# A mixture-of-experts layer on one core: the residual is loaded in the expert stage and biased by VectorE, every pair has its own buffer, and the stores go out on GpSimd's queue

## The reference

```python
def _L0_cond_ref(x, q_left, q_right, spectral_gate):   # a linear map on the channels of each token
    ...
def _L0_ffn_ref(x, W_in, b_in, W_gate, b_gate, W1, b1, W2, b2, W_out, b_out):
    h = x @ W_in + b_in
    t = h.reshape(B * S, -1)
    logits = t @ W_gate + b_gate
    probs = jax.nn.softmax(logits, axis=-1)
    topv, topi = jax.lax.top_k(probs, TOP_K)
    topv = topv / jnp.sum(topv, axis=-1, keepdims=True)
    route = jnp.zeros_like(probs).at[jnp.arange(t.shape[0])[:, None], topi].set(topv)
    mid = jax.nn.relu(jnp.einsum('nd,edh->neh', t, W1) + b1)
    eout = jnp.einsum('neh,ehd->ned', mid, W2) + b2
    moe_out = jnp.einsum('ne,ned->nd', route, eout)
    out = moe_out.reshape(B, S, -1) @ W_out + b_out
    return out
x = x + _L0_ffn_ref(_L0_cond_ref(x, ...), ...)
```

## Time and profile before

| what | value |
|---|---|
| time, median of 3 runs | 589.87 us (589.3 to 590.82) |
| the profiled execution | 589.61 us, of which the span from the first to the last instruction is 587.8 us |
| TensorE busy | 535.3 us (91%) |
| VectorE, ScalarE, GpSimd busy | 354.5, 300.9 and 240.7 us |
| bytes moved | 64.70 MB, mean 110 GB/s |

### The profile page before, as it was taken

How to read it: one execution, slowest core, us unless ns; L and a number is a source line. 1 busy time by engine, 2 the same in 40 slices (tenths; PEclk the granted TensorE clock), 3 DMA queues, 4 the chain that set the end, 5 groups by cost and what they waited for, 6 DMA issues and landing times.

```text
span 587.8 us, 14218 instructions
## 1 busy us (share of the span) xinstructions
PE 535.3 (91%) x4458; PEld 463.9 (79%) x4459; DVE 354.5 (60%) x696; ACT 300.9 (51%) x534; POOL 240.7 (41%) x291
## 2 busy tenths in 40 slices
PE   1999947899999999999999999999999999963887
PEld 1666826798998998898998998998899988852665
DVE  5359643675774774774784784774564554625754
ACT  1266554765565565565665665663543543503443
POOL 3012235073373472473482472472432433229400
PEclk9899986999999999999999999999999999995999
DMA  6506362051251251251251241111111121195695
GB/s 163 171 19 241 110 218 77 18 192 54 64 180 55 71 179 46 80 167 49 86 164 45 94 154 48 48 55 42 55 55 38 55 55 38 38 321 180 209 293 178
DMA packets 40359, 64.70 MB, mean 110 GB/s; under 512 B 5943, under 2 KB 28156, under 8 KB 40316
## 3 DMA queue, kind: packets, MB, share of 16 engines
q1 hardware_dynamic: 31548, 39.51, 20.9%
q0 software_dynamic: 8768, 24.65, 13.4%
HBM read 45.53 MB, written 18.61 MB: 109 GB/s over the span
## 4 chain that ended last, share of the span: by engine, by line
PE 81%; DMA 7%; DVE 3%; ACT 2%; issue 2%; SPq 2%; POOL 2%; POOLq 1%; DVEq 0%; ACTq 0%
PE bank L1027 33%; PE bank L1010 12%; PE bank L1012 12%; PE bank L1011 12%; PE bank L909 4%; DMA w1s<-in_x 3%; PE bank L991 3%; DMA w1s<-y_by_choice 2%; POOL w1s L451 2%; PE bank L1060 1%; PE bank L891 1%; DVE w1s L855 1%; PE bank L881 1%; DMA z_by_token<-w1s 1%; PE bank L918 1%
## 5 line engine op out<-in xcount | busy, mean ns | idle before, releaser
L545 ACT ACTIVATE region<-bank,b1p,cbits 128x256 f32<-128x256 f32 x312 | 158.8, 560 | 184.5 <-PE bank L1012 168.3
L1027 PE MATMUL bank<-w2s,region 128*128 x1872 | 210.6, 273 | 0.0
L1027 PEld LDWEIGHTS bank<-w2s,region 128*128 128x128 f16 x1872 | 183.2, 98 | 20.8
L1010 PE MATMUL bank<-region,w1s 128*128 128x256 f16 x624 | 171.1, 274 | 0.3 <-DVE region L799 0.3
L1011 PE MATMUL bank<-region,w1s 128*128 128x256 f16 x624 | 171.0, 274 | 0.0
L1012 PE MATMUL bank<-region,w1s 128*128 128x256 f16 x624 | 171.0, 274 | 0.0
L429 POOL DMA_INDIRECT y_by_choice<-region,dst x78 | 84.8, 1087 | 208.2 <-DVE region L810 192.4
L820 DVE CAST region<-region 128x512 f16<-128x512 f32 x156 | 66.7, 428 | 78.5 <-ACT region L545 74.3
L822 DVE TENSOR_TENSOR region<-region 128x512 f16<-128x512 f32 x156 | 108.0, 692 | 5.4
L422 POOL DMA_INDIRECT region<-z_by_token,src x78 | 77.6, 995 | 28.4 <-issue 23.6
L810 DVE SCALAR_TENSOR_TENSOR region<-bank,cbits,b2b 128x256 f32<-128x256 f32 x78 | 34.1, 479 | 76.0 <-PE bank L1027 76.0
(11 more groups left out here) (194 smaller groups left out, 434.2 us busy)
## 6 DMA issues: line engine op xcount, KB each, us to landing
region<-in_L_ffn_W SPq DMA_DIRECT2D x16, 1024.0 KB
w1s<-y_by_choice SPq DMA_DIRECT2D x16, 512.0 KB, 4.3
w1s<-in_x SPq DMA_DIRECT2D x8, 512.0 KB, 8.6
z_by_token<-w1s POOLq DMA_DIRECT2D x16, 256.0 KB, 2.9
w1s<-in_x SPq DMA_DIRECT2D x4, 1024.0 KB, 9.9
out<-w1s SPq DMA_DIRECT2D x16, 256.0 KB, 2.6
region<-z_by_token,src POOLq DMA_INDIRECT x78, 2.8
y_by_choice<-region,dst POOLq DMA_INDIRECT x78, 2.6
```

Source lines behind the costliest of these rows:

```text
L545: m = s.activation(midf[:, b, c * TS:(c + 1) * TS], FB[b][:, c * TS:(c + 1) * TS], ACT.Relu, bias=b1p[:, bass.ds(r, 1), f:f + 1].rearrange ...
L1010: mm(o, w, xs[:, par, 0, k, :], start=(k == 0), stop=False)
L1027: last = mm(YB[par][:, h * D:(h + 1) * D], mids[:, par, l, b, c * TS + h * P:c * TS + (h + 1) * P], w2_at(e, w, f), start=(f == 0 and l == ...
```

## The change

x is loaded by SyncE as soon as the last weights are converted and 17 tiles have passed the second layer (`load_residual`). The four MB go to space that is free by then: the two raw weight buffers, and the weights of the rank that was computed first, in `w1s` and `w2s`. VectorE adds b_out in place, two pairs behind each of the tiles 30 to 37 (`add_bias`). All 16 pairs have their own buffers in the rest of `w1s` and `w2s`, and SyncE issues all 16 loads one after the other when the rows are scattered. GpSimd issues the stores. The loops of the output stage are written out.

```diff
+        def pairs(i):
+            at = fin1[:, i * SF:(i + 1) * SF] if i < NF1 else fin2[:, (i - NF1) * SF:(i - NF1 + 1) * SF]
+            return at.rearrange("p (t k d) -> p t k d", t=CT, k=K)
...
+        XC = NT // 4
+        xres = [region[:, RR:RR + XC * D], region[:, RR + XC * D:RR + 2 * XC * D],
+                w1s[:, 0].bitcast(f32).rearrange("p l k f -> p (l k f)"),
+                w2s[:, 0].bitcast(f32).rearrange("p l k f -> p (l k f)")]
...
+        XB0 = 30
...
-            sp.wait_ge(s_mp, 4 * NTILE)
-            for c in range(4):
-                t = slice(c * NT // 4, (c + 1) * NT // 4)
-                sp.dma_start(xall[:, t], x_t[:, t, :]).then_inc(s_xf, 16)
+            def load_residual():
+                sp.wait_ge(s_wl, 4 * E)
+                sp.wait_ge(s_yp, N // TS + 1)
+                for c in range(4):
+                    sp.dma_start(xres[c].rearrange("p (t d) -> p t d", t=XC), x_t[:, c * XC:(c + 1) * XC, :]
+                                 ).then_inc(s_xf[c], 16)
+            load_residual()
             sp.wait_ge(s_sc[0], 16 * H * ((NTILE + 1) // 2))
             sp.wait_ge(s_sc[1], 16 * H * (NTILE // 2))
-            for i in range(SL):
-                sp.dma_start(yin[:, i], y_t[:, i * CT:(i + 1) * CT]).then_inc(s_yi[i], 16)
-            with sp.Fori(0, NS // SL - 1) as j:
-                for q in range(SL):
-                    load(j * SL + (q + SL), q)
-                    store(j * SL + q)
-            for i in range(NS - SL, NS):
-                store(i)
+            for i in range(NS):
+                sp.dma_start(pairs(i), y_t[:, i * CT:(i + 1) * CT]).then_inc(s_yi[i], 16)
             sp.wait_ge(s_st, 16 * NS)
...
-            pool.wait_ge(s_late, 16 * 2)
-            pool.wait_ge(s_xf, 16 * 4)
-            combine(pool, add_bias)
+            for i in range(NS):
+                pool.wait_ge(s_o, i + 1)
+                pool.dma_start(out_t[:, i * CT:(i + 1) * CT, :], residual(i)).then_inc(s_st, 16)
...
+            def add_bias(i):
+                c, q = divmod(i, NS // 4)
+                if q == 0:
+                    dve.wait_ge(s_xf[c], 16)
+                v.tensor_tensor(residual(i), residual(i), bc(boutb[:].unsqueeze(1), [P, CT, D]), ALU.add
+                                ).then_inc(s_xb, 1)
...
             for a in range(NTILE):
                 tile(a, a % 2, a // GT)
+                for i in range(2 * (a - XB0), 2 * (a - XB0) + 2):
+                    if 0 <= i < NS:
+                        add_bias(i)
```

More of the change, by code:

```diff
@@ L249, in moe_program @@
         s_sc = [sem(f"rows_scattered{i}") for i in range(2)]
-        s_yi = [sem(f"pairs_loaded{i}") for i in range(SL)]
+        s_yi = [sem(f"pairs_loaded{i}") for i in range(NS)]
         s_y1 = sem("first_choice_scaled")
@@ L258, in moe_program @@
         s_o = sem("out_ready")
-        s_xf = sem("residual_loaded")
+        s_xf = [sem(f"residual_loaded{i}") for i in range(4)]
         s_st = sem("out_stored")
@@ L291, in tiles, with combine @@
                 step(a, a % 2, a // GT, a % GT)
-        def combine(eng, step):
-            for i in range(SL):
-                step(i, i, 0)
-            with eng.Fori(1, NS // SL) as j:
-                for q in range(SL):
-                    step(j * SL + q, q, j)
+        def combine(step):
+            for i in range(NS):
+                step(i, i % 2)
+        XB0 = 30
         @block.sync
@@ L837, in _ @@
             dve.wait_ge(s_tab, 1)
+            dve.wait_ge(s_late, 16 * 2)
             for a in range(NTILE):
                 tile(a, a % 2, a // GT)
+                for i in range(2 * (a - XB0), 2 * (a - XB0) + 2):
+                    if 0 <= i < NS:
+                        add_bias(i)
             y_out(NTILE - 1, 0)
@@ L844, in finish, with mix @@
                 dve.wait_ge(s_xb, i + 1)
-                t = bass.ds(i * CT, CT)
-                v.tensor_tensor(xall[:, t], bank[2 + par][:].rearrange("p (t d) -> p t d", t=CT), xall[:, t],
+                v.tensor_tensor(residual(i), bank[2 + par][:].rearrange("p (t d) -> p t d", t=CT), residual(i),
                                 ALU.add).then_inc(s_o, 1)
-            def mix(i, slot, j):
-                dve.wait_ge(s_yi[slot], (j + 1) * 16)
+            def mix(i, par):
                 dve.wait_ge(s_y1, i + 1)
-                if later(i, 2):
+                if i >= 2:
                     dve.wait_ge(s_zp, i - 1)
                 for t in range(CT):
-                    last = v.scalar_tensor_tensor(ztok[:, slot % 2, t, :], yin[:, slot, t, 1, :],
-                                                  route[:, 1, bass.ds(i * CT + t, 1)], y1r[:, slot % 2, t, :],
+                    last = v.scalar_tensor_tensor(ztok[:, par, t, :], pairs(i)[:, t, 1, :],
+                                                  route[:, 1, i * CT + t:i * CT + t + 1], y1r[:, par, t, :],
                                                   ALU.mult, ALU.add)
                 last.then_inc(s_z, 1)
-                if later(i, 2):
-                    finish(i - 2, slot % 2)
-            combine(dve, mix)
+                if i >= 2:
+                    finish(i - 2, par)
+            combine(mix)
             finish(NS - 2, 0)
@@ L1062, in project, with mix_t @@
                 last.then_inc(s_op, 1)
-            def mix_t(i, slot, j):
+            def mix_t(i, par):
                 pe.wait_ge(s_z, i + 1)
-                if later(i, 2):
+                if i >= 2:
                     pe.wait_ge(s_zt, i - 1)
@@ L1069, in mix_t @@
                     for k in range(KD):
-                        last = tr(bank[slot % 2][:, (t * KD + k) * P:(t * KD + k + 1) * P],
-                                  ztok[:, slot % 2, t, k * P:(k + 1) * P], ident[:])
+                        last = tr(bank[par][:, (t * KD + k) * P:(t * KD + k + 1) * P],
+                                  ztok[:, par, t, k * P:(k + 1) * P], ident[:])
                 last.then_inc(s_zp, 1)
-                if later(i, 1):
-                    project(i - 1, (slot + 1) % 2)
-            combine(pe, mix_t)
+                if i >= 1:
+                    project(i - 1, 1 - par)
+            combine(mix_t)
             project(NS - 1, (NS - 1) % 2)
```

45 lines of the change are left out of this document (19 added, 26 removed).

## The result

The changed kernel takes 580.84 us, the median of 5 runs (577.28 to 581.17), against 589.87 for the kernel before (588.55 to 590.82). The ratio is 0.984, with a 95% interval of 0.981 to 0.988: 9.0 us less in medians. Some executions of a kernel are slower as a whole, and medians and ratios leave them out (six of 22 of the kernel before, beside the first four experiments). The profiled execution is the fastest of the five, at 577.28, with a span of 575.5.

The account below looks back on a forecast made before the run. TensorE, busy for 535.3 of 587.8 us, was taken as the bound. Start 3.95 and pace 6.27 us less, last store 0.3 more, gave a span of 577.9, as a median 580.0; predicted 579.8, range 577.0 to 584.0.

Parts of the forecast that it names:

- the start: Output stage: the first finish comes 3.95 us earlier, at 541.05 instead of 545.00.
- the pace: Output stage: TensorE paces finishes at 2.22 us instead of 2.64, so 15 steps take 33.3 us, 6.27 less.
- the end: From the last finish to the end of the span: 2.84 us instead of 2.54, 0.3 more.
- The x load costs nothing: Expert stage: the early x load beside gathers and scatters costs 0, with 3.4 us of cover for a slow gather.
- The additions cost nothing: Expert stage: two VectorE additions per tile, 0.69 us each, fit in 1.48 us of idle time; cost 0.
- The hole: TensorE's idle time before the output stage: first transposes start 2.4 us earlier, at 535.2, second ones 3.95 us earlier.
- The clock's rise: Output stage: TensorE's clock rises to full 4.4 us after the second transposes start, at 540.9.
- The DMA rival: Second half of the output stage: DMAs set the pace, giving 582.3 or 584.4 us; chance 0.19.
- The stores on GpSimd: Output stage: issues take 0.73 us and only the last store's time counts, 0.3 us more at the end.
- The rival that was slower than before: Output stage: GpSimd paces the stores at 3.7 us each, held up by VectorE, giving 605 us; chance 0.04.
- the sum: Whole output stage: 3.95 and 6.27 us won, 0.3 lost, 9.9 us less than 587.8.

Follow-up runs that it names:

- the first four experiments: Changed kernel unedited (583.40 us), with stores on SyncE (577.99), with only the early x load kept (583.97), with only the queued loads kept (584.65).
- bias4_sp: stores_sp with four additions on VectorE behind each of tiles 30 to 33 instead of two behind 30 to 37: 576.11 us, ratio 0.977.
- bias_pool_mid: stores_sp with the additions on GpSimd, two behind the gathers in each of tiles 30 to 37: 583.54 us, ratio 0.984.
- x_early_only: Changed kernel with loads back in the closed loop, four ahead, and stores on SyncE; early x load and VectorE's additions stay: 583.97 us, ratio 0.990.
- stores_sp: Changed kernel with all 16 stores issued by SyncE behind the 16 loads: 577.99 us, ratio 0.979.
- pool_late_memset: stores_sp with a GpSimd memset of a two-column tile after the last finish: 578.44 us, ratio 0.981.
- last4_sp: Changed kernel with the last four stores on SyncE and the first twelve still on GpSimd: 578.36 us, ratio 0.978.
- bias_pool_tail: stores_sp with the 16 additions on GpSimd after its last scatter, x still loaded early: 589.19 us, ratio 0.999.
- second profile: Profile of the changed kernel run once more, unedited: median 583.40 us, ratio 0.989, output stage 54.5 us.

## Why the prediction was right, and where it was not

The forecast of 579.8 was 1.0 off the median of 580.84, inside the range, and the start and the pace came as forecast. That it is so close is in part luck: up to the end of the last finish the profile won 1.2 us more than forecast, the end lost 3.7 more, and the five runs spread over 3.9 us. The steps, against the profile of the changed kernel:

*The x load costs nothing: right.* It moved beside gathers and scatters (304 GB/s from 390 to 402), the worst gather landed 6.4 us after its issue, where 6.3 had been taken, and TensorE had no wait for one. (The load's end was put a microsecond late: 388.24 + 11.7 is 399.9, not 401, which changes nothing.)

*The additions cost nothing: right.* One takes 0.68 us, for which 0.69 was taken. bias4_sp doubled them, and bias_pool_mid showed what the place costs on the other engine.

*The hole: right.* First transposes 10.55 us after the last second layer (predicted 10.9), second 11.9 (12.2), first finish 16.4 (16.75). The gain of 3.95 us was 4.3. The clock's rise, 4.4 us after the second transposes in the sum, was 5.3 in one profile and 2.0 in another of the same kernel: a term with a scatter of a microsecond or two that I treated as fixed.

*The pace: right, 0.8 us too slow* over 15 steps (2.165 against 2.22). TensorE's own step is 2.16 without waits.

*The DMA rival rested on a wrong reading.* I divided 304 GB/s by a share of 0.94 and called 320 GB/s full. The changed kernel moved 408, and the last load had landed at 552.0. The share is the time packets are under way; in a closed loop with four loads ahead they are slow ones (x_early_only: 0.95 at 296 GB/s). The 0.19 that I gave this rival was too much.

*The stores on GpSimd: the step that failed.* I predicted that "only the last one's time counts", 0.3 us more at the end. It was 4.0 more: 6.54 us from the last finish's end to the end of the span, against 2.54. The store itself landed in 2.5 us at best and 2.7 in the median, and no issue took more than 0.79, so neither the landing nor the descriptors were the cause: GpSimd's closing drain was, which stores_sp, pool_late_memset and last4_sp showed. I had the rows in reach. In the profile before, GpSimd's additions ended at 551.0 and its drain at 555.0, 4 us later, where nothing waited for it:

```profile
529.75 21.27 POOL L451 TENSOR_TENSOR w1s<-w1s,boutb 128x512 f32<-128x512 f32 x16 [1.88 <-DMA w1s<-in_x]
```

```profile
L44 POOLq DRAIN  x1: 20203/20203/20203, 534.8 to 534.8; - x1
```

*The rival that was slower than before* needed 2.74 us per store on GpSimd; the issues took 0.71. VectorE's instructions there do not hold up a store's issue. But the same two engines do hold each other up when GpSimd computes, and by far more than the 1.0 us per instruction that I priced from before: 13.8 us in bias_pool_tail. The Trainium skill (SBUF — State Buffer, section "Who interferes with whom") lets a VectorE instruction with two SBUF inputs block beside a GpSimd one that reads SBUF, and the trace agrees: the mixes are such instructions, and the additions held them up. The section has the port held for one whole instruction; in bias_pool_tail the mix waited for eleven, and there the measurement decides.

So in the output stage the sum was 9.9 and the measured gain 7.4 (9.0 in the second profile): +0.3 at the start, +0.8 in the pace, -3.7 at the end. That the medians differ by 9.0 and not 7.4 is within what the earlier stages scatter.

## What to carry to other kernels

Measure a change from a mark that the untouched stages cannot move, here the end of the last second layer, before reading a difference of two profiles. A high DMA share is no proof of full DMA engines: look at what the same traffic reaches when more of it is queued. Let no GpSimd work be the last thing in a kernel, and do not let GpSimd compute beside a VectorE that others wait for; what went to it for free here were DMA issues, the last of which ended 7 us ahead of the end of the last finish (last4_sp).

## What was unexpected of the hardware

- GpSimd's drain at the end of the program ends 4.0 us after its last instruction in the eleven profiles where that is an addition, a memset or the issue of a scatter, and 5.0 to 5.3 us after it in the three where it is the issue of a store (the changed kernel twice, last4_sp). Why it is that long is open.
- One VectorE instruction of 0.48 us waited for 13.76 us, through eleven GpSimd instructions that followed each other, in bias_pool_tail; in three other kernels with the same instructions the two took turns at about 1.4 us each. In bias_pool_mid a cast waited for two additions in the same way. What decides between the two is open.
- Loads of 2 KB rows and stores together moved 408 GB/s from 545 to 550 with 16 loads queued, and 296 to 344 with four ahead.
- TensorE's clock rose to full 2.0 and 5.3 us after the start of the second transposes in two profiles of the changed kernel, and 4.4 us after it in the profile before.
